# Draining a fused decoder layer: where the shared expert's pieces, the last routing groups and the packet sends stand

## The chip, the cores and the metric

One core of one Trainium2 chip. The metric is device time of one launch in microseconds (us): the kernel before took 727.16 us as the median of 3 runs (726.34 to 728.71). The core has five engines that run side by side and wait for each other through semaphores: TensorE (PE, matmuls; its weight loads are listed as PEld), VectorE (DVE), ScalarE (ACT), GpSimd (POOL) and SyncE (SP). SP, ACT and POOL start DMAs.

## The reference, cut to what matters

`x` is 32 sequences (B) of 128 rows (S) of 256 channels (D), all float32.

```python
x = layernorm(x + self_attention(x))          # 16 heads of 16 channels, causal
x = layernorm(x + retention(x, ctx))          # rotated q and k, decay mask, no softmax
hs = silu(x @ sw1[:, :256] + b) * (x @ sw1[:, 256:] + b)      # the shared expert, for every row
shared = hs @ sw2 + sb2
probs = softmax(x @ gate_w + gate_b)          # 8 experts; each row takes the best 2
routed = sum over the row's 2 experts of  p_e * expert_e(x)   # same shape as the shared expert
x = layernorm(x + shared + routed)
```

## The kernel before, in words

**Attention steps.** A token block `t` is one of the 32 sequences (128 rows). Both attentions run in a software pipeline of steps `n`. In step `n` each engine handles several blocks at different stages: scores and softmax of block n, weighing of the values and first layernorm of block n-2 (result `x1`), keys, values and queries of the second attention for block n-3 (`K_TURNED`, `XV`, `Q_TURNED`; VectorE makes `products` of them, GpSimd adds these to `rot`), its 128x128 scores `SCX` and its output `YX` for n-4 with the second layernorm (`packets`, that is x2), and for n-5 the turned x2 (`x2T`) and its gate logits (`GATE`, added up to `gc`). From step 32 = B on no new block comes, and the steps run out: step 32 is the first without scores, step B+4 = 36 the last with any attention work. The order of instructions on each engine is the order in which the `step` functions write them; there is no planner.

**Routing groups.** Blocks are gated in `GROUPS`: seven groups of 4 (q0 to q6: blocks 0 to 27), then two of 2 (q7: 28 and 29, q8: 30 and 31). A group's VectorE work has four parts (L1556 to L1562): largest and lowered logits; sums and top two probabilities; top two experts and `picks`; `places` and `positions`. `groups_at(n, lag)` gives the groups whose part `lag` stands in step n: part 0 in `group_step(q)`, which is 32, 34 and 36 for q6, q7 and q8, and each further part one step later, so `places` of q8 stands in step 39. TensorE computes the group's prefix counts (L996 to L1004) in the step of `places`. `places` also moves `base`, the next free row of each expert's region in the HBM tensor `sent`; only after q8 is it final.

**Sending.** GpSimd scatters each block's packets (x2 and routing data) with two indirect DMAs per block to `sent` (L641). `sent_at(n)` sends one block per step, for blocks up to 27; the pairs 28, 29 and 30, 31 go in steps 38 and 40. The sends stand in front of the step's `rot` additions and of the layernorms' `rstd` (L650, L654).

**Shared expert.** Rows 0 to 15 (four quarters q of 4 blocks, `EARLY`) go through the shared expert here. `shared_hidden(q, f, bank)` is 4 matmul calls of 512 columns in two halves (a and b) in PSUM banks `bank` and `bank+1`; ScalarE makes silu of one half, VectorE `shared_gate` (L1452) the product, then `shared_output(q, ...)` has 8 calls of 256 columns and `add_shared` (L1463) adds the result to `kept`. `shared_between(n)` lays one of these pieces into each of steps 33 to 39 on TensorE, in the middle of the step: hidden(0,0), (0,1), (1,0), output 0, hidden (1,1), (2,0), output 1. Behind the loop come hidden (2,1), (3,0), (3,1) and outputs 2 and 3. Each engine has its own `shared_between`.

**Behind the steps.** VectorE makes `tail_rows` from `base` and then a plan of 15 small steps (`tile_expert`, `tile_row`), with one `shared_gate` in the middle. After `tail_rows` SP and ACT write 128 zero rows behind each expert's region (5 and 3 DMAs). SP waits for the plan, for all sends and for the zero rows (L550 to L554); then it starts the loads of the routed tiles: tile i reads 128 packets from `sent` into `xg`. There are 71 tiles. Per tile TensorE turns `xg` (L1038), makes the hidden layer (L1051) and the result of the tile before (L1060). SP also stores `kept` (L547) between the loads of tiles 2 and 3. A last stage joins everything, makes the shared expert of the other rows and the third layernorm.

Of the kernel before, what the change touches and what calls it, by code (L numbers as in the profile page):

```python
# [14 lines left out]
P = 128  # L15
# [71 lines left out]
def groups_at(n, lag):  # L87
    return [q for q in range(len(GROUPS)) if group_step(q) + lag == n]


def sent_at(n):

    return [lo + j for q, (lo, size) in enumerate(GROUPS) for j in range(size)
            if group_step(q) + 4 + (j if size == 4 else 0) == n]


def decoder_kernel(nc, x, ctx_turned, wqkv, xwq, xwk, xwv, gate_w, gate_b, sw1, sb1, sw2, sb2,
                   rw1, biases, rw2, table_f32, table_bf16, x_turned, x_blocks, out):
    ctx = ExitStack()
    with ctx:  # L100
# [26 lines left out]
        GATE = ps[:, 7, D:D + NE]  # L127
        PREFIX = ps[:, 7, D + NE:D + 5 * NE].rearrange("p (b e) -> p b e", e=NE)
# [279 lines left out]
        FIRST_STEP, END_STEP = -2, group_step(len(GROUPS) - 1) + 5  # L408
# [190 lines left out]
        def _(eng):  # L599
# [17 lines left out]

            def step(n):
# [18 lines left out]
                for t in sent_at(n):  # L637
                    eng.wait_ge(pos_set, group_of(t) + 1)
                    eng.wait_ge(scored, 4 * min(n + 1, B))
                    for j in range(TOPK):  # L640
                        eng.indirect_dma_start(sent, bass.IndirectOffsetOnAxis(ap=pos[:, t, j:j + 1], axis=0),  # L641
                                               packets[:, t % SLOTS, :], None).then_inc(sent_in[t % SLOTS], 16)
# [92 lines left out]
        def _(eng):  # L735
# [96 lines left out]
            def shared_hidden(q, f, bank):  # L832
                if q > 0:
                    eng.wait_ge(sgh_set, 2 * (q - 1) + f + 1)
                for half in range(2):
                    shared_half(q, f, half, bank)

            def shared_output(q, *banks):

                eng.wait_ge(sgh_set, 2 * q + 2)  # L840
                for i, bank in enumerate(banks):
                    if 0 < q < EARLY - 1:
                        eng.wait_ge(sy_added, 2 * (q - 1) + i + 1)
                    for b in (2 * i, 2 * i + 1):
                        for c in range(FFN // P):
                            mm = eng.matmul(ps[:, bank, b % 2 * D:(b % 2 + 1) * D], sgh[:, q % 2, c, b * P:(b + 1) * P],
                                            sw2_sb[:, c, :], start=(c == 0), stop=(c == FFN // P - 1))
                    mm.then_inc(sy_made, 1)

            def shared_between(n):  # L850

                if n == B + 1:
                    eng.wait_ge(ffn_in, 16 * (2 + 2 * NE))
                    eng.wait_ge(expd, 4 * B)
                    shared_hidden(0, 0, 0)
                if n == B + 2:
                    shared_hidden(0, 1, 2)
                if n == B + 3:
                    shared_hidden(1, 0, 0)
                if n == B + 4:  # L860
                    eng.wait_ge(pT_set, 4 * B)
                    eng.wait_ge(att_set, B)
                    shared_output(0, 4, 5)
                if n == B + 5:
                    shared_hidden(1, 1, 2)
                if n == B + 6:
                    shared_hidden(2, 0, 0)
                if n == B + 7:
                    shared_output(1, 4, 5)
# [7 lines left out]
            def step(n):  # L877
# [20 lines left out]
                if live(t):  # L898
# [4 lines left out]
                    eng.wait_ge(x1T_set, t + 1)  # L903
# [19 lines left out]
                if live(t):  # L923
# [4 lines left out]
                    else:  # L928
                        eng.wait_ge(res2_set, n - 4)
                    for m in range(2):  # L930
# [16 lines left out]
                shared_between(n)  # L947
# [26 lines left out]
                if live(n - 1):  # L974
                    turn_probs(n - 1, 3)
                t = n - 5
# [8 lines left out]
                if n == 0:  # L985
# [4 lines left out]
                    project_k(NG - 1, 0, 5)  # L990
                for q in groups_at(n, 3):
# [15 lines left out]
                if live(t):  # L1007
# [4 lines left out]
                    after(eng, gc_set, n - 4)  # L1012
                    for c in range(DC):
                        mm = eng.transpose(TR[:, c * P:(c + 1) * P], x1[:, t % 2, c * P:(c + 1) * P], ident)
# [8 lines left out]
            shared_hidden(2, 1, 2)  # L1023
            shared_hidden(3, 0, 0)
# [88 lines left out]
        def _(eng):  # L1113
# [23 lines left out]
            def shared_between(n):  # L1137
                if n == B + 1:
                    eng.wait_ge(heads_made, B)
                    shared_silu(0, 0, 0)  # L1140
                if n == B + 2:
                    shared_silu(0, 1, 2)
                if n == B + 3:
                    shared_silu(1, 0, 0)
                if n == B + 5:
                    shared_silu(1, 1, 2)
                if n == B + 6:
                    shared_silu(2, 0, 0)

            def step(n):  # L1150
# [26 lines left out]
                shared_between(n)  # L1177
# [13 lines left out]
                if live(t):  # L1191
                    eng.wait_ge(x1_turned, t + 1)
                    after(eng, xq_made, t - 1)
                    eng.copy(x1T[:, t % 2, :, :].rearrange("p c t -> p (c t)"), TR).then_inc(x1T_set, 1)
# [15 lines left out]
            shared_silu(2, 1, 2)  # L1210
# [103 lines left out]
        def _(eng):  # L1314
# [150 lines left out]
            def shared_between(n):  # L1465
                if n == B + 1:
                    shared_gate(0, 0, 0)
                if n == B + 2:
                    shared_gate(0, 1, 2)
                if n == B + 3:  # L1470
                    shared_gate(1, 0, 0)
# [299 lines left out]
```

## Time and profile before

| | |
|---|---|
| median of 3 runs | 727.16 us |
| the profiled execution | 723.76 us |
| its span in the trace | 721.7 us |
| PE, DVE, ACT, POOL busy | 683.2, 489.2, 478.9, 343.1 us |
| matmul records of the routed tiles, L1051 and L1060 | 138.9 and 74.9 us |

The profiled execution is 2.06 us longer than its span and 3.40 us shorter than the median. Times in the trace count from the start of the span. A float32 matmul call stands as two records, so a `shared_hidden` is 8 records and a `shared_output` 16. "Busy" of PE counts records, which overlap a little. A gap ahead of an instruction is given in brackets with the instruction that ended it.

### The profile page before, as it was taken

To read this page: it belongs to the slowest core of one execution; us is meant where nothing else is said; L and a number is where in the kernel's file an instruction comes from. 1 tells how busy PE (TensorE), PEld (TensorE's weight loads), DVE (VectorE), ACT (ScalarE), POOL (GpSimd) and SP (SyncE) were. 2 spreads that over 40 slices of the span, in tenths; PEclk is the share of its full clock that TensorE was granted. 3 is DMA by queue.
4 is the path that set the end of the run, shared out by engine and by line. 5 is a ranking of instruction groups with operands and counts; after the bars stand their busy time and mean duration, and the time that the engine had idled before them with its cause. 6 is when DMAs were issued, how large, how long until landed. Compare 5 with 4: busy or idle time off the path is not lost.

```text
span 721.7 us, 21540 instructions
## 1 busy us (share of the span) xinstructions
PE 683.2 (95%) x6174; PEld 588.5 (82%) x6175; DVE 489.2 (68%) x1563; ACT 478.9 (66%) x1319; POOL 343.1 (48%) x469
## 2 busy tenths in 40 slices
PE   7989999999999999999998899889999999999994
PEld 5868888888888888888887555779999999998653
DVE  3666878888888888888896376445555555554266
ACT  0367888888888888888884242356666666666256
POOL 1001323435645455454455355055665556556495
PEclk9999999999999999999999899999999999999998
DMA  8743367424523233232336024686777777777597
GB/s 306 236 146 114 116 204 240 137 88 147 158 88 96 67 91 105 86 107 83 104 97 198 31 89 143 198 221 126 140 134 139 133 139 136 135 137 130 124 349 261
DMA packets 93947, 104.30 MB, mean 145 GB/s; under 512 B 13200, under 2 KB 86672, under 8 KB 92976
## 3 DMA queue, kind: packets, MB, share of 16 engines
q1 hardware_dynamic: 78480, 79.43, 37.2%
q0 software_dynamic: 14688, 23.26, 16.4%
q8 instruction: 40, 0.66, 0.4%
q10 hardware_dynamic: 704, 0.66, 0.3%
q14 instruction: 35, 0.29, 0.1%
HBM read 62.21 MB, written 41.10 MB: 143 GB/s over the span
## 4 chain that ended last, share of the span: by engine, by line
PE 78%; DVE 5%; DMA 5%; POOL 4%; issue 4%; SPq 3%; ACT 1%; DVEq 0%; POOLq 0%; ACTq 0%
PE ps L1051 15%; PE ps L1060 8%; PE ps L806 6%; PE ps L908 5%; PE ps L794 5%; PE ps L816 4%; PE ps L771 4%; PE ps L739 4%; PE ps L911 4%; PE ps L774 4%; PE ps L932 4%; DMA xg<-sent 3%; POOL first_use L715 2%; PE ps L1038 2%; PE ps L826 2%
## 5 line engine op out<-in xcount | busy, mean ns | idle before, releaser
L1118 ACT ACTIVATE prob<-ps,nmax 128x128 f32<-128x128 f32 x512 | 147.0, 380 | 27.4 <-DVE nmax L1332 27.4
L1051 PEld LDWEIGHTS ps<-xgT,attn_only 128*128 128x128 f32 x1136 | 136.0, 192 | 7.4 <-DVE ghT L1614 2.2
L1051 PE MATMUL ps<-xgT,attn_only 128*128 128x128 f32 x1136 | 138.9, 275 | 1.1 <-ACT xgT L1230 1.1
L674 POOL DMA_INDIRECT total<-rot,result_row x71 | 111.6, 1572 | 36.8 <-issue 34.3
L1332 DVE TENSOR_REDUCE nmax<-ps 128x4 f32<-128x512 f32 x128 | 82.2, 685 | 17.7 <-PE ps L794 17.0
L1614 DVE SCALAR_TENSOR_TENSOR ghT<-ps,attn_only 128x128 f32<-128x128 f32 x142 | 43.3, 347 | 71.0 <-PE ps L1051 59.3
L615 POOL TENSOR_TENSOR rot<-products 128x128 f32<-128x128 f32 x128 | 61.3, 499 | 57.1 <-DVE products L1342 57.0
L1125 ACT COPY pT<-ps 128x512 f32<-128x512 f32 x124 | 74.4, 600 | 20.8 <-PE ps L806 16.4
L806 PE MATMUL ps<-tf,prob 128*128 128x128 f32 x512 | 77.9, 275 | 4.4 <-DVE pT L1447 3.3
L641 POOL DMA_INDIRECT sent<-packets,pos x64 | 63.6, 993 | 35.6 <-PE ps L794 20.9
L1060 PE MATMUL ps<-first_use,ghT 128*128 x284 | 74.9, 386 | 0.0
L806 PEld LDWEIGHTS ps<-tf,prob 128*128 128x128 f32 x512 | 58.7, 140 | 11.0 <-issue 4.9
L1238 ACT COPY attn_only<-first_use 128x512 f32 x71 | 44.0, 619 | 28.4 <-issue 28.4
L826 PE MATMUL ps<-prob,sw_sb 128*128 128x512 f32 x128 | 56.8, 594 | 0.0
L1230 ACT COPY xgT<-ps 128x256 f32<-128x256 f32 x71 | 26.5, 373 | 44.7 <-PE ps L1038 43.9
L1060 PEld LDWEIGHTS ps<-first_use,ghT 128*128 128x128 f32 x284 | 48.4, 190 | 6.0 <-issue 0.5
L1342 DVE TENSOR_TENSOR products<-ps,tf 128x256 f32<-128x256 f32 x128 | 46.4, 404 | 6.7 <-PE ps L911 2.3
L1603 DVE COPY attn_only<-first_use 128x512 f32 x71 | 31.2, 439 | 28.4 <-issue 28.0
L654 POOL TENSOR_TENSOR rstd<-mv,neg_half 128x1 f32<-128x1 f32 x32 | 17.7, 552 | 67.0 <-DVE mv L1350 67.0
L1224 ACT ACTIVATE attn_only<-ps,attn_only 128x128 f32<-128x128 f32 x142 | 44.2, 361 | 7.6 <-PE ps L1051 4.8
L662 POOL TENSOR_TENSOR weight<-weight_part,xg 128x1 f32<-128x1 f32 x71 | 13.4, 188 | 70.4 <-ACT rot L1244 49.9
L826 PEld LDWEIGHTS ps<-prob,sw_sb 128*128 128x128 f32 x128 | 23.9, 190 | 26.0 <-issue 25.6
(143 smaller groups left out, 1408.1 us busy)
## 6 DMA issues: line engine op xcount, KB each, us to landing
xg<-sent SPq DMA_DIRECT2D x71, 130.5 KB, 2.1
attn_only<-in_L_ffn_rb SPq DMA_DIRECT2D x71, 130.0 KB
first_use<-total SPq DMA_DIRECT2D x12, 512.0 KB, 8.7
total<-zeros POOLq DMA_DIRECT2D x3, 1408.0 KB, 8.0
k_dram<-first_use SPq DMA_DIRECT2D x4, 1024.0 KB, 4.6
attn_only<-in_x_turned SPq DMA_DIRECT2D x32, 128.0 KB, 2.5
attn_only<-k_dram SPq DMA_DIRECT2D x256, 16.0 KB
attn_only<-in_x SPq DMA_DIRECT2D x32, 128.0 KB, 2.7
```

The costliest lines, as they stand in the source:

```text
L615: eng.tensor_tensor(rot[:, t % 2, m + e, :], ra[:, t % 2, m + e, :], rb[:, t % 2, m + 1 - e, :], ALU.add).then_inc(done, 1)
L641: eng.indirect_dma_start(sent, bass.IndirectOffsetOnAxis(ap=pos[:, t, j:j + 1], axis=0), packets[:, t % SLOTS, :], None).then_inc(sent_in[ ...
L674: eng.indirect_dma_start(totals[slot % 2], bass.IndirectOffsetOnAxis(ap=result_row[:, slot:slot + 1], axis=0), yw[:, slot, :], None, compu ...
L806: mm = eng.transpose(PROBT[:, n * P:(n + 1) * P], prob[:, t % 2, 4 * u + n, :], ident)
L826: mm = eng.matmul(ps[:, bank + half, :].rearrange("p (b t) -> p b t", b=QB), sw1_sb[:, c, cols:cols + P], x2T4[:, q % EARLY, :, c, :], sta ...
L1051: mm = eng.matmul(ps[:, 2 * r + half, f * P:(f + 1) * P], w_now[:, r, c, cols:cols + P], xgT[:, r, c, :], start=(c == 0), stop=(c == DC - 1))
L1060: mm = eng.matmul(ps[:, 4 + r, 0:D], ghT[:, r, c, :], rw2_sb[:, bass.ds(e * (FFN // P * D) + c * D, D)], start=(c == 0), stop=(c == FFN // ...
L1118: ins = eng.activation(prob[:, t % 2, 4 * u + n, :], SCORE[u][:, n * P:(n + 1) * P], ACT.Exp, bias=nmax[:, t % 2, 4 * u + n:4 * u + n + 1])
L1125: eng.copy(pT[:, u, :, :].rearrange("p n t -> p (n t)"), PROBT).then_inc(pT_set, 1)
L1224: eng.activation(sil[:, r, f, :], ps[:, 2 * r, f * P:(f + 1) * P], ACT.Silu, bias=side[:, slot, f:f + 1]).then_inc(sil_set, 1)
L1332: eng.tensor_reduce(nmax[:, t % 2, 4 * u:4 * u + 4], SCORE[u].rearrange("p (h j) -> p h j", j=P), AX_X, ALU.max, negate=True).then_inc(max ...
L1342: eng.tensor_tensor(into[:, t % 2, m:m + 2, :], source, table[:, m:m + 2, :], ALU.mult).then_inc(done, 1)
```

## The change

Three things are moved; the arithmetic stays the same, and so does the number of matmuls, gating operations, silus and sends.

1. **Groups.** For q6, q7 and q8 the parts stand 0, 1, 1 and 2 steps behind `group_step`: the second and third part share a step, `places` and the prefix counts come in steps 34, 36 and 38 (before 35, 37, 39). The loop ends one step earlier.
2. **Sends.** Blocks 20 and 21 are sent in step 32, 22 and 23 in 33, 24 and 25 in 34, 26 and 27 in 35, 28 and 29 in 36, 30 and 31 in 38. From step 34 on the sends stand at the end of GpSimd's step, behind `rot` and `rstd`.
3. **Pieces of the shared expert.** TensorE gets two places per step: `shared_upper` behind SCX, where `shared_between` stood, and `shared_lower` behind the gate logits. Halves a and b of one hidden piece are parted. So hidden(0,0) stands in step 32; hidden (0,1), (1,0), (1,1) each have one half up and one down in steps 33, 34, 35; output 0 stands in step 36 in two parts, one of them between the turning of x2 and the gate logits; hidden(2,0) in 36 and 37, (2,1) in 37 and 38; output 1 and hidden(3,0) in 39. Behind the loop only hidden(3,1) and outputs 2 and 3 are left. On ScalarE the silu moves behind the x1 copy, on VectorE the gate product moves ahead of the second residual sum, and in the plan `add_shared(1)` and `shared_gate(3, 0, 0)` stand where `shared_gate(2, 1, 2)` stood. The turned x1 of blocks 30 and 31 goes to PSUM bank 4 instead of bank 7, so it no longer waits for the gate logits, and the step's waits are changed to match.

```diff
+QUICK = len(GROUPS) - 3
+LAST_SENT = {B: (20, 21), B + 1: (22, 23), B + 2: (24, 25), B + 3: (26, 27), B + 4: (28, 29), B + 6: (30, 31)}
 def groups_at(n, lag):
-    return [q for q in range(len(GROUPS)) if group_step(q) + lag == n]
+    return [q for q in range(len(GROUPS)) if group_step(q) + (lag if q < QUICK else (0, 1, 1, 2)[lag]) == n]
 def sent_at(n):
-    return [lo + j for q, (lo, size) in enumerate(GROUPS) for j in range(size)
-            if group_step(q) + 4 + (j if size == 4 else 0) == n]
+    if n < B:
+        return [t for t in (n - 12,) if 0 <= t < LAST_SENT[B][0]]
+    return LAST_SENT.get(n, ())
...
-        FIRST_STEP, END_STEP = -2, group_step(len(GROUPS) - 1) + 5
+        FIRST_STEP, END_STEP = -2, group_step(len(GROUPS) - 1) + 4
...
 # GpSimd: send(n) holds the old loop over sent_at(n)
+                if n < B + 2:
+                    send(n)
...
+                if n >= B + 2:
+                    send(n)
...
 # TensorE
+            def shared_first(q, f, bank):
+                if q > 0:
+                    eng.wait_ge(sgh_set, 2 * (q - 1) + f + 1)
+                shared_half(q, f, 0, bank)
+            def shared_rows(q, i, bank):
+                eng.wait_ge(sgh_set, 2 * q + 2)
+                if 0 < q < EARLY - 1:
+                    eng.wait_ge(sy_added, 2 * (q - 1) + i + 1)
+                for b in (2 * i, 2 * i + 1):
+                    for c in range(FFN // P):
+                        mm = eng.matmul(...)
+                mm.then_inc(sy_made, 1)
+            def shared_upper(n):
                 if n == B + 1:
+                    shared_first(0, 1, 2)
+                if n == B + 2:
+                    shared_first(1, 0, 0)
+                if n == B + 3:
+                    shared_first(1, 1, 2)
+                if n == B + 4:
+                    eng.wait_ge(pT_set, 4 * B)
+                    eng.wait_ge(x1T_set, B)
+                    eng.wait_ge(att_set, B)
+                    shared_rows(0, 0, 4)
+                if n == B + 5:
+                    shared_half(2, 0, 1, 0)
+                    shared_first(2, 1, 2)
+                if n == B + 6:
+                    shared_half(2, 1, 1, 2)
+                if n == B + 7:
+                    shared_output(1, 4, 5)
+                    shared_hidden(3, 0, 0)
+            def shared_lower(n):
+                if n == B:
                     eng.wait_ge(ffn_in, 16 * (2 + 2 * NE))
                     eng.wait_ge(expd, 4 * B)
                     shared_hidden(0, 0, 0)
+                if n == B + 1:
+                    shared_half(0, 1, 1, 2)
                 if n == B + 2:
+                    shared_half(1, 0, 1, 0)
                 if n == B + 3:
+                    shared_half(1, 1, 1, 2)
                 if n == B + 4:
+                    shared_first(2, 0, 0)
...
-                    eng.wait_ge(x1T_set, t + 1)
+                    if t < B - 2:
+                        eng.wait_ge(x1T_set, t + 1)
+                    else:
+                        eng.wait_ge(gc_set, n - 5)
...
+                if n == B + 4:
+                    shared_rows(0, 1, 5)
...
-                        mm = eng.transpose(TR[:, c * P:(c + 1) * P], x1[:, t % 2, c * P:(c + 1) * P], ident)
+                        mm = eng.transpose(turned_x1(t)[:, c * P:(c + 1) * P], x1[:, t % 2, c * P:(c + 1) * P], ident)
...
-            shared_hidden(2, 1, 2)
-            shared_hidden(3, 0, 0)
             shared_hidden(3, 1, 2)
...
 # VectorE, in the plan behind the loop
-            shared_gate(2, 1, 2)
+            add_shared(1, 4, 5)
+            shared_gate(3, 0, 0)
```

## Rows read from the trace of the kernel before

**Rows 1.** Windows: engines' busy us (records), granted clock, DMA share, GB/s.

```profile
391.20:404.20 13.00, 10.22 (x79) 6.91 (x77) 6.49 (x22) 4.16 (x8) 6.08 (x10) 0.96 0.41 139
404.20:410.20 6.00, 6.00 (x24) 5.62 (x25) 3.20 (x13) 0.37 (x1) 3.57 (x5) 0.52 0.19 68
410.20:422.40 12.20, 10.71 (x46) 5.58 (x45) 6.26 (x31) 4.73 (x7) 4.09 (x7) 1.00 0.15 54
422.40:437.90 15.50, 15.04 (x63) 9.91 (x61) 8.97 (x47) 4.53 (x6) 10.94 (x12) 1.00 0.27 96
437.90:455.25 17.35, 17.35 (x61) 10.74 (x60) 12.02 (x29) 3.28 (x5) 5.79 (x6) 1.00 0.48 138
```

**Rows 2.** Chain that ended last, around the first routed tiles: start, us, what.

```profile
438.75 1.28 DVE kept L1463 x2
440.03 0.37 DVE tail_rows L1578
447.20 3.46 DMA sent<-zeros
450.80 0.28 SPq L561
...
462.41 3.34 DMA xg<-sent
```

**Rows 3.** Timeline of TensorE: start, us, line, operation, gap and its releaser.

```profile
390.75 0.41 PE L1014 MATMUL ps<-tf,x 128*128 128x128 f32 x2 [1.27 <-DVE gc L1543]
396.13 3.60 PE L826 MATMUL ps<-prob,sw_sb 128*128 128x512 f32 x8
402.11 0.61 PE L981 MATMUL ps<-gate_w_sb,x2T 128*128 128x8 f32 x4 [1.73 <-ACT x2T L1183]
...
437.86 0.17 PE L996 MATMUL ps<-picks,tb 128*128 128x16 bf16 x1
...
448.35 7.07 PE L846 MATMUL ps<-sw_sb,sgh 128*128 128x256 f32 x32
455.25 0.38 PE L1038 MATMUL ps<-tf,xg 128*128 128x128 f32 x2
...
465.79 0.44 PE L1038 MATMUL ps<-tf,xg 128*128 128x128 f32 x2 [1.85 <-DMA xg<-sent]
```

**Rows 4.** Timeline of ScalarE (first row) and VectorE: the same columns.

```profile
399.81 1.28 ACT L1135 ACT_TABLE_LOAD   x1 [5.27 <-PE ps L826]
...
404.19 0.18 DVE L1366 TENSOR_REDUCE gsum<-gexp 128x4 f32<-128x32 f32 x1
405.45 0.73 DVE L1452 SCALAR_TENSOR_TENSOR sgh<-ps,sb_sb,pT 128x512 f32<-128x512 f32 x1
...
417.70 0.08 DVE L1389 MATCH_VALUE_LOAD top_i<-top_p,gprob 128x8 f32 x1
...
418.95 0.19 DVE L1413 TENSOR_TENSOR picks<-pick 128x32 bf16<-128x32 f32 x1
```

**Rows 5.** GpSimd: L641's durations (ns) and landings (us), then its timeline.

```profile
L641 POOL DMA_INDIRECT sent<-packets,pos x64: 959/970/1076, 161.9 to 444.5; - x64
DMA to landing us min/median/max: 2.5/3.1/5.8
...
416.02 0.57 POOL L654 TENSOR_TENSOR rstd<-mv,neg_half 128x1 f32<-128x1 f32 x1 [4.62 <-DVE mv L1350]
...
425.41 1.02 POOL L641 DMA_INDIRECT sent<-packets,pos  x1 [1.26 <-DVE pos L1436]
...
444.53 0.97 POOL L641 DMA_INDIRECT sent<-packets,pos  x1 [0.30 <-issue]
```

**Rows 6.** Timeline: GpSimd and VectorE side by side, and VectorE with GpSimd sending.

```profile
392.04 0.73 POOL L635 TENSOR_TENSOR x2b<-packets,sb_sb 128x256 f32<-128x256 f32 x1 [0.53 <-DVE packets L1555]
392.09 0.73 DVE L1360 TENSOR_TENSOR gs<-gc,lmax 128x32 f32<-128x32 f32 x1
...
427.86 0.18 DVE L1360 TENSOR_TENSOR gs<-gc,lmax 128x16 f32<-128x16 f32 x1
```

More of the change, by code:

```diff
@@ L616, in turn_into, with send @@
                                       ALU.add).then_inc(done, 1)
+            def send(n):
+                for t in sent_at(n):
+                    eng.wait_ge(pos_set, group_of(t) + 1)
+                    eng.wait_ge(scored, 4 * min(n + 1, B))
+                    for j in range(TOPK):
+                        eng.indirect_dma_start(sent, bass.IndirectOffsetOnAxis(ap=pos[:, t, j:j + 1], axis=0),
+                                               packets[:, t % SLOTS, :], None).then_inc(sent_in[t % SLOTS], 16)
             def step(n):
@@ L636, in step @@
                                       sb2_sb[:, :], ALU.add).then_inc(x2b_set, 1)
[L637 to L642, printed above, removed]
+                if n < B + 2:
+                    send(n)
                 t = n - 3
@@ L830, in shared_half, with shared_hidden @@
                     mm.then_inc(shid_made, 1)
-            def shared_hidden(q, f, bank):
+            def shared_first(q, f, bank):
                 if q > 0:
                     eng.wait_ge(sgh_set, 2 * (q - 1) + f + 1)
-                for half in range(2):
-                    shared_half(q, f, half, bank)
+                shared_half(q, f, 0, bank)
+            def shared_hidden(q, f, bank):
+                shared_first(q, f, bank)
+                shared_half(q, f, 1, bank)
+            def shared_rows(q, i, bank):
[4 more added lines that the diff above has]
+                    for c in range(FFN // P):
+                        mm = eng.matmul(ps[:, bank, b % 2 * D:(b % 2 + 1) * D], sgh[:, q % 2, c, b * P:(b + 1) * P],
+                                        sw2_sb[:, c, :], start=(c == 0), stop=(c == FFN // P - 1))
+                mm.then_inc(sy_made, 1)
@@ L838, in shared_output @@
             def shared_output(q, *banks):
-                eng.wait_ge(sgh_set, 2 * q + 2)
                 for i, bank in enumerate(banks):
[L842 to L848, printed above, removed]
@@ L850, in shared_between @@
-            def shared_between(n):
-                if n == B + 1:
+                    shared_rows(q, i, bank)
+            def shared_upper(n):
+                if n == B + 1:
+                    shared_first(0, 1, 2)
[16 more added lines that the diff above has]
+                    shared_hidden(3, 0, 0)
@@ L1193, in step @@
                     after(eng, xq_made, t - 1)
-                    eng.copy(x1T[:, t % 2, :, :].rearrange("p c t -> p (c t)"), TR).then_inc(x1T_set, 1)
+                    eng.copy(x1T[:, t % 2, :, :].rearrange("p c t -> p (c t)"), turned_x1(t)).then_inc(x1T_set, 1)
+                shared_between(n)
                 if live(n) and live(n + 1):
@@ L1474, in shared_between @@
                 if n == B + 5:
-                    shared_gate(1, 1, 2)
+                    shared_gate(2, 0, 0)
                 if n == B + 6:
-                    shared_gate(2, 0, 0)
-                if n == B + 7:
-                    add_shared(1, 4, 5)
+                    shared_gate(2, 1, 2)
             def step(n):
@@ L1523, in step @@
                     eng.bn_stats(bn1[:, r2, :], res1[:, r2, :]).then_inc(bn1_set, 1)
+                if n == B + 1:
+                    shared_gate(0, 0, 0)
+                if n == B + 2:
+                    shared_gate(0, 1, 2)
+                if n == B + 3:
+                    shared_gate(1, 0, 0)
+                if n == B + 4:
+                    shared_gate(1, 1, 2)
                 if live(t4):
```

48 lines of the change are left out of this document (20 added, 28 removed).

## The prediction

> **What bounds the kernel now.** I read the windows first: where does TensorE lose time? Behind step 31 it loses it in one place only, the running out of the steps. From 391.20 to 404.20 it is busy 10.22 of 13.00 us; from 404.20 to 410.20 it is busy throughout, but its clock was granted at 0.52, so it ran at the lower of its two levels (1.2 of 2.4 GHz) after a stretch with long gaps; from 410.20 to 422.40 it is busy 10.71 of 12.20; from 422.40 on it has almost no gap, and from 437.90 to 455.25 none [rows 1]. Then the timeline of TensorE, for what ended these gaps: 1.27 us for the logits' copy in front of the turned x1, 1.73 us for a turned x2 [rows 3]. ScalarE made that x2 late because it had waited 5.27 us for a whole hidden piece and then loaded an activation table for 1.28 us [rows 4].
>
> Last the chain of waits, for what the routed tiles wait for. It does not run through TensorE. It runs from `places` of the last group over `add_shared(1)` (1.28 us), `tail_rows` (ends 440.40), SP's zero rows (the last one starts at 447.20 and lands 3.46 us later) to the first load, which SP begins at 450.80, and on to tile 3, whose packets land at 465.79 [rows 2]. TensorE ends its own shared pieces at 455.25 and goes on without a gap, but at tile 3 it stands 1.85 us for SP's load [rows 3]. So two paths meet: TensorE's, with 1.85 us of slack at tile 3, and SP's, which sets the start of the routed tiles. Behind tile 3 the change touches nothing, and a shift there passes to the end.
>
> **The change part by part.** *Work on TensorE.* A hidden piece takes 3.46 us: three fill 437.96 to 448.35 (one alone is 8 records, 3.60 us with its drain); an output takes 3.45, since two fill 448.35 to 455.25 [rows 3]. In front of the prefix counts of q8 stood five hidden pieces and two outputs; now six and one. That is the same work. What can go is only lost time: gaps of 1.27, 2.78, 1.49 and 0.46 us, plus 0.48 of 6.0 us and 0.04 of 13.0 us for the clock, 3.4 us; 9.4 us in all [rows 1, 3]. This is the upper bound of TensorE's gain.
>
> *New waits.* I laid the new order by hand, instruction by instruction, with the durations of this trace, from 389.4, where the logits of block 27 end and hidden(0,0) now follows. Its input landed before that. It runs to 392.9, over the old gap of 1.27. Four things then cost:
> - Steps 32 and 33 send two blocks each: two more sends each, at 1.27 us from start to start (970 ns and 0.30 of idle [rows 5]), so `rot` and `rstd` stand 2.5 us further back in GpSimd's queue. In step 32 this makes x1 of block 30 1.3 us late, which hidden(0,0) covers; in step 33 the additions for block 30 end at 401.3 and TensorE asks for them at 406.
> - In step 33 the second and third part of q6 stand together on VectorE, 1.26 and 1.44 us (404.19 to 405.45, 417.70 to 419.14 [rows 4]). They end at 407.0, and the products of block 31 stand behind them. TensorE is ready for SCX of block 30 at 406.05 and starts at 407.85: a gap of 1.8 us.
> - Prefix counts of q6 end at 413.45; the next SCX shares their bank and waits for `base`, 1.05 us.
> - In step 34 the sends of blocks 24 and 25 start with q6's positions at 415.0 (before: 425.41 [rows 5]) and hold GpSimd to 420.1. The last `rstd` of all, for block 31, is ready to start at 418.8 but now has these sends and the x2 sum in front: it runs 420.9 to 421.45 (0.57 us [rows 5]). TensorE stands 0.55 us for x2 of block 31, and VectorE's q7 chain ends at 424.1, before TensorE asks at 426.25.
>
> With 0.5 us of short waits TensorE loses 3.9 us where it lost 9.4: 5.5 us less. The schedule itself puts the prefix of q8 at 431.75, against 437.86 [rows 3]: 6.1 less. I take the middle, 5.8. The parted outputs in step 36 and the late silus cost nothing: each gate product is asked for one step after it is made, and the halves between cover it.
>
> *SP's path.* Behind `positions` of q8 stood `add_shared(1)`, 1.28 us; now stands a gate product of 0.75 us [rows 2, 4]. So `tail_rows` comes 5.8 + 0.5 = 6.3 us earlier, at 434.1. Three things must not be late next. The plan: its middle now waits for silu(3,0), whose matmuls end at 438.9; with silu 0.7, product 0.75 and five more steps of 2.2 us it ends at 442.5. The sends: before, 16 of them ran in one chain from 425.41 to 445.5; now only four follow the last positions, 432.9 to 438.0, and with the longest landing seen, 5.8 us [rows 5], they are in at 443.8. The zero rows: 440.40 to 450.66 becomes 434.1 to 444.4 [rows 2]. The zero rows stay last, by 0.6 us.
>
> *End of the shared pieces.* Behind the loop three pieces instead of five; with the pieces of step 39 TensorE reaches the first routed tile near 449.5, 5.8 us earlier. It would ask for tile 3 at 458.1; SP's load lands at 465.79 - 6.3 = 459.5. SP's stores of `kept` need `add_shared(3)`, at 450.7; SP comes to them at 451.1.
>
> **Sum.** SP's path sets the start: 6.3 us, of which I take 6.2 for the near tie of the stores. The profiled execution took 723.76 us (span 721.7), so one like it takes 717.6 (715.5). The median of the runs lies 3.40 us above that execution; from it, 727.16 - 6.2 = **721.0 us**.
>
> *A rule against it.* VectorE's lowering of logits took 0.73 us while GpSimd's sum was running, and 0.18 (at half the size) while GpSimd was only sending [rows 6]; the 64 sends took 959 to 1076 ns, whatever VectorE did [rows 5]. The Trainium skill (SBUF — State Buffer, "Who interferes with whom") says that VectorE and GpSimd take one shared port pair as an exclusive lock, and that descriptors of a DMA sent by GpSimd can't be written while VectorE holds it in a two-port mode. The first row agrees. On sends the trace speaks against a loss; by the rule, sends moved beside VectorE's busiest steps would stretch, which is part of the first rival.
>
> **Rivals.**
> - *GpSimd becomes the bound.* The four sends in front of the last `rstd` are on the path. If each is held for one VectorE operation of 0.73 us, that is 2.9 us: 723.9. For it: only these sends have no slack, and my 415.0 hangs on q6's positions. Against it: 64 sends within 0.12 us of each other [rows 5]. The skill's port rule, in the page named above, is one way to it.
> - *Waits move, they don't go.* VectorE, not TensorE, becomes the clock of steps 33 to 36, since its groups got denser; my 3.9 us of loss doubles and adds the clock's 2.9 again. Gain 6.2 - 3.9 - 2.9 below zero is the far end; with the doubling and half of the clock it is 0.8: 726.4, no change.
> - *All gaps fill.* If VectorE keeps up and GpSimd's sends start earlier, TensorE loses about 1 us: gain 8.9 with the 0.5, and the sends (slack 0.6 us against the zero rows) then limit it near 8.5: 718.7.
> - *Slower: the clock falls in step 34.* The trace shows it once: 0.96 to 404.20, with the gap of 1.73 us and shorter ones in it, then 0.52 for 6 us [rows 1, 3]. The new order has its longest gap, 1.8 us, at 406. If the clock falls there and stays low for the 9.0 us of matmuls of step 34 and the start of 35, those take 18: 721.0 + 9.0 = 730.0. It decides from 8.4 us of such work on (6.2 and the 0.3% below). Against it: between the gaps the halves of the shared pieces now stand, and before, 1.27 us alone did not lower the clock.
>
> That it doesn't do what it says I see no room for.
>
> **How the numbers follow.** Forecast 0.56 (its own range 719.4 to 723.0), GpSimd 0.13, waits that move 0.10, all gaps 0.12, slower 0.09. A difference under 0.3%, 2.2 us, can't be told from none. Faster by more: 0.56 + 0.13 + 0.12, 0.81. Same 0.10; slower 0.09. For 8 in 10 the range must hold the first two cases and most of the third: 717.5 to 725.0.
>
> **What would show it.** Right: `tail_rows` about 6 us earlier, near 434; first load 6 us earlier; clock at 1.00 through 404 to 410; a gap near 1.8 us ahead of SCX in step 34 with VectorE's products as releaser; `rstd` of block 31 directly behind four sends; still a gap at tile 3. Wrong: a stretch at 0.5 clock, `tail_rows` later than 437, or a first load that now waits for sends or plan rather than zero rows. If tile 3 starts 6 us earlier but the end does not, the routed stage took the gain back.

## The result and the profile after

The changed kernel took **721.69 us** as the median of 8 runs (720.38 to 724.33), the kernel before, on the same chip, 727.54 (724.37 to 729.93): ratio 0.9912, 95% interval 0.9887 to 0.9937. The forecast was 721.0. Two more measurements of the same pair gave 0.9873 (0.9838 to 0.9907) and 0.9878 (0.9842 to 0.9914). The profiled execution took 721.88 us, span 719.9.

The windows of TensorE answer to [rows 1]; the columns are length, busy us (records), granted clock, DMA share, GB/s.

```profile
380.00:390.00 10.00, 8.56 (x86) 0.83 0.63 182
390.00:400.00 10.00, 8.71 (x73) 1.00 0.56 187
400.00:410.00 10.00, 7.58 (x36) 1.00 0.16 56
410.00:420.00 10.00, 8.60 (x51) 1.00 0.08 27
420.00:430.00 10.00, 9.44 (x43) 1.00 0.27 95
430.00:440.00 10.00, 10.00 (x39) 1.00 0.35 124
```

The stretch at half clock at 404 to 410 is gone; in its place stands a shorter fall at 383 to 387, in front of the change's steps. TensorE's timeline answers to [rows 3]:

```profile
382.72 0.18 PE L1042 MATMUL ps<-picks,tb 128*128 128x32 bf16 x1 [1.44 <-DVE gc L1593]
...
392.26 0.41 PE L1005 MATMUL ps<-tf,packets 128*128 128x128 f32 x2 [1.29 <-DVE scx L1556]
402.31 0.66 PE L959 MATMUL ps<-tf,oT 128*128 128x128 f32 x4 [1.70 <-issue]
404.55 0.68 PE L988 MATMUL ps<-rot 128*128 128x128 f32 x4 [0.69 <-DVE products L1392]
414.26 0.68 PE L988 MATMUL ps<-rot 128*128 128x128 f32 x4 [1.33 <-DVE products L1392]
420.53 0.68 PE L988 MATMUL ps<-rot 128*128 128x128 f32 x4 [0.57 <-DVE base L1474]
427.63 0.44 PE L1005 MATMUL ps<-tf,packets 128*128 128x128 f32 x2
...
454.55 0.38 PE L1087 MATMUL ps<-tf,xg 128*128 128x128 f32 x2
464.80 0.44 PE L1087 MATMUL ps<-tf,xg 128*128 128x128 f32 x2 [1.76 <-DMA xg<-sent]
```

Only the gaps of 1.33, 0.57 and 1.76 us were in the forecast. Then VectorE, SyncE and the chain of waits (its piece `sent<-zeros`), which answer to [rows 2]:

```profile
438.72 0.22 DVE L1628 TENSOR_SCALAR tail_rows<-base,tf 128x8 uint32<-128x8 f32 x1
444.96 0.69 DVE L1513 TENSOR_TENSOR kept<-ps,kept 128x512 f32<-128x512 f32 x1 [2.09 <-remote]
448.42 0.22 DVE L1647 TENSOR_TENSOR tile_row<-tile_f,tf 1x71 int32<-1x71 f32 x1
...
440.53 7.23 SPq L551 DMA_DIRECT2D sent<-zeros  x5
450.30 0.37 SPq L571 DMA_DIRECT2D xg<-sent  x1
...
447.42 2.00 DMA sent<-zeros
```

`tail_rows` came 1.2 us earlier than before, not 6; tile 3 by 1.0. Yet the runs had gained 6. So this trace, or the one of before, held something that is not the change. To compare traces I count from one fixed place ahead of the change, the prefix counts of q5 (first line of the TensorE rows; 380.93 in the first trace of before, 382.72 here).

### The profile page after: what moved, and what is told of

The parts are those of the page before. It is cut to its first block, busy times and chain, and to the rows that moved or that the text cites. A ratio compares the mean times of both kernels' runs of the same rounds, so it can differ in the third digit from the quotient of the medians.

```text
span 719.9 us, 21546 instructions
## 1 busy us (share of the span) xinstructions
PE 682.0 (95%) x6174; PEld 587.2 (82%) x6175; DVE 488.0 (68%) x1563; ACT 478.6 (66%) x1319; POOL 342.8 (48%) x469
## 4 chain that ended last, share of the span: by engine, by line
PE 73%; issue 7%; DMA 5%; DVE 5%; POOL 4%; SPq 3%; ACT 1%; another core or an unknown queue 1%; DVEq 0%; POOLq 0%; ACTq 0%
PE ps L1100 15%; PE ps L1109 8%; PE ps L821 6%; PE ps L809 5%; PE ps L949 5%; PE ps L831 4%; PE ps L786 4%; PE ps L789 4%; PE ps L975 4%; PE ps L952 4%; PE ps L754 3%; DMA xg<-sent 2%; POOL first_use L730 2%; PE ps L1087 2%; PE ps L959 2%
## 5 line engine op out<-in xcount | busy, mean ns | idle before, releaser
L667 POOL TENSOR_TENSOR rstd<-mv,neg_half 128x1 f32<-128x1 f32 x32 | 17.6, 549 | 62.5 <-DVE mv L1400 62.5
L663 POOL TENSOR_TENSOR rstd<-mv,neg_half 128x1 f32<-128x1 f32 x32 | 18.0, 562 | 54.1 <-DVE mv L1400 54.1
```

## Experiments

Twelve measurements. The first four and the last four ran on one chip, the middle four on another; which one ran the first result isn't known. Each has its own ratio to before from the same chip, and only ratios are compared between chips (the expected times of experiments 5 to 8 were written with the first result's 721.7 in mind). This table counts from the prefix counts of q5, us. "Stall" is a stretch, at some 430 to 450, in which SyncE, VectorE and ScalarE go on late, all at once (experiment 5 and the last section):

| kernel | to tail_rows | to tile 3 | clock low at 382 to 388 | stall |
|---|---|---|---|---|
| before, first trace | 59.0 | 84.9 | no | no |
| before, second trace | 62.9 | 88.0 | no | yes |
| changed, first | 56.0 | 82.1 | yes | yes |
| changed, second | 52.5 | 78.0 | yes | no |
| changed, third | 56.1 | 82.1 | yes | yes |
| pieces alone, twice (1, 11) | 51.0; 53.0 | 81.5; 83.3 | no; yes | yes; yes |
| pieces, plan first (12) | 51.0 | 81.0 | no | yes |
| pieces and groups (4) | 58.5 | 83.5 | no | yes |
| experiments 6; 8 | 52.5; 52.5 | 76.6; 78.5 | yes; yes | no; no |
| experiment 7 | 50.9 | 75.1 | no | no |

**1. Only the pieces.** The new places of the shared expert's halves and bank 4, with the groups and sends of before. Against the changed kernel:

```diff
 def groups_at(n, lag):
...
+    return [q for q in range(len(GROUPS)) if group_step(q) + lag == n]
...
-                if n == B + 7:
-                    shared_output(1, 4, 5)
-                    shared_hidden(3, 0, 0)
...
+            shared_output(1, 4, 5)
+            shared_hidden(3, 0, 0)
             shared_hidden(3, 1, 2)
```

> Only the third part of the change: the shared expert's halves in their new places and the turned x1 of blocks 30 and 31 in bank 4; groups and sends as before. Output 1 and hidden(3,0) stand behind the loop, so that the prefix counts of the last group have the same work in front of them as in both kernels (six hidden pieces, one output). Theory A (the gain is TensorE's lost time in steps 32 to 36, filled by the halves): 5 to 6.5 us faster than before, ratio 0.991 to 0.993, first gap in step 34 smaller than with the dense groups. Theory B (the gain is that the last group is gated a step earlier): no gain, ratio 0.998 to 1.002.

Measured: 721.44 us, 0.9894 (0.9871 to 0.9917): the whole effect, from one of the three parts, and a little more than theory A's 0.991 to 0.993. The gap ahead of SCX in step 34 is 0.57 us where the changed kernel has 1.33, as theory A says.

**2. Only the groups.** Against the kernel before:

```diff
 def groups_at(n, lag):
-    return [q for q in range(len(GROUPS)) if group_step(q) + lag == n]
+    return [q for q in range(len(GROUPS)) if group_step(q) + (lag if q < QUICK else (0, 1, 1, 2)[lag]) == n]
```

> Only the first part: q6, q7 and q8 gated in fewer steps; pieces and sends as before. Theory A: tail_rows still stands behind add_shared(1) and output 1, so nothing comes earlier, and VectorE's denser steps cost up to 1.8 us: ratio 1.000 to 1.003. Theory B: prefix counts stand one output (3.45 us) earlier, about 3 us faster, ratio 0.995 to 0.997.

Measured: 737.81 us, 1.0111 (1.0078 to 1.0145), slower, which neither theory had. TensorE's timeline and its windows:

```profile
421.79 1.19 PE L947 MATMUL ps<-rot 128*128 128x128 f32 x4 [2.08 <-DVE base L1426]
422.77 5.71 PE L828 MATMUL ps<-prob,sw_sb 128*128 128x512 f32 x8
...
416.00:422.00 6.00, 3.19 (x21) 0.85 0.06 22
422.00:428.00 6.00, 6.00 (x12) 0.58 0.21 69
```

The prefix counts now stand directly in front of SCX, which waits for `base`; behind that gap a hidden piece takes 5.71 us where it took 3.60 [rows 3], at a granted clock of 0.58.

**3. Groups and sends, no pieces.** Experiment 2 and, besides:

```diff
 def sent_at(n):
+    if n < B:
+        return [t for t in (n - 12,) if 0 <= t < LAST_SENT[B][0]]
+    return LAST_SENT.get(n, ())
...
+                if n >= B + 2:
+                    send(n)
```

> First and second part without the third. Theory A: no gain over groups alone; with no half behind the logits of step 32, the two more sends there (2.5 us) delay x1 of block 30 in the open by 1.3 us: ratio 1.000 to 1.004. Theory B: 3 to 6 us faster, ratio 0.992 to 0.996. A third theory, that the late sends held the first load, also says faster here, by up to 3 us.

Measured: 727.75 us, 0.9984 (0.9959 to 1.001). The second fall of the clock stays (a hidden piece of 5.91 us behind a gap of 1.61). Without the pieces the other two parts give nothing, as theory A said.

**4. Pieces and groups, old sends.** The changed kernel with the `sent_at` of before and all sends in front of `rot` and `rstd`:

```diff
-                if n < B + 2:
-                    send(n)
+                send(n)
...
-                if n >= B + 2:
-                    send(n)
```

> The change without its second part: the sends stay one block a step, the last at the end. Theory A: the last 16 sends then run as one chain of 20.3 us from step 36 on (about 426) and end near 446, with 3 to 5 us to land: later than the zero rows by 4 us or more, so the first load waits for sends and the kernel is 3 to 5 us slower than the changed one, ratio to before 0.996 to 1.000. Rival (the sends have slack in any order): as the changed kernel, ratio 0.991 to 0.993.

Measured: 724.59 us, 0.994 (0.9916 to 0.9964). This lies between theory A's range and the rival's, and the trace doesn't show theory A's cause, a first load that waits for sends. The loss stands ahead of `tail_rows`, 58.5 us behind q5's counts: TensorE's prefix counts of q8 ended at 432.2, and VectorE's `place`, which needs them, began only at 438.97, in the stall. The clock is at 1.00 from 382 on: with the halves in place the gaps of 1.33 and 0.97 us ahead of the two SCX do not lower it. The theory that the earlier gating of the last groups brings the gain (theory B of experiments 1 to 3) has fallen; that the pieces bring it stands.

**5. The changed kernel again, unchanged.**

> The changed kernel once more, unchanged, for its trace. Open: in its first trace, while GpSimd's sends ran, SyncE, VectorE and ScalarE all slowed down at once (SyncE's zero rows 7.23 us of issuing where the kernel before took 5.74; add_shared(1) waited 2.09 us for a semaphore; the plan ended 9.7 us behind tail_rows where 8.4 was forecast). Theory S (the order of sends and zero rows in this kernel causes it): it stands at the same place, 441 to 445 us, zero rows 6.9 to 7.5 us of issuing, median 721 to 722. Theory C (it is a chance event of one execution): the zero rows take 5.6 to 6.0 us here, or the stall lies elsewhere; from tail_rows to the first load 10.4 us (before) instead of 11.6, and the profiled execution is 1 to 2 us shorter than the first one's 719.9 us of span.

Measured: 715.12 us, 0.9873. VectorE, SyncE and TensorE, in this order:

```profile
433.37 0.22 DVE L1628 TENSOR_SCALAR tail_rows<-base,tf 128x8 uint32<-128x8 f32 x1
442.42 0.22 DVE L1647 TENSOR_TENSOR tile_row<-tile_f,tf 1x71 int32<-1x71 f32 x1
434.99 5.43 SPq L551 DMA_DIRECT2D sent<-zeros  x5
444.19 0.37 SPq L571 DMA_DIRECT2D xg<-sent  x1
408.96 0.68 PE L988 MATMUL ps<-rot 128*128 128x128 f32 x4 [1.34 <-DVE products L1392]
449.19 0.38 PE L1087 MATMUL ps<-tf,xg 128*128 128x128 f32 x2
458.86 0.44 PE L1087 MATMUL ps<-tf,xg 128*128 128x128 f32 x2 [1.17 <-DMA xg<-sent]
```

This order of instructions can run without the stall (theory C): the zero rows take 5.43 us of issuing, not 7.23, and `add_shared(1)` no longer waits. But this is another chip, and experiment 10 has the stall again. The profiled execution took 717.93 us, 2.8 above the median of its kernel.

**6. Tile 3's load first.** `load(3, 3)` stands ahead of the four `store_kept`.

```diff
+            load(3, 3)
             for q in range(EARLY):
                 store_kept(q)
-            load(3, 3)
```

> SyncE issues the load of tile 3 before the four stores of kept blocks that stood in front of it. Theory: tile 3's gap of 1.76 us on TensorE ends with that load; the stores before it cost SyncE their wait for add_shared(3) and four issues, some 1.5 us. With the load first, the gap falls below 0.4 us and the time by 1.0 to 1.8 us: 720 beside 721.7. Rival: the stores are not what the load waits for (its packets land late because the queue is full of the loads of tiles 0 to 2, 3.46 us each): the gap stays above 1.3 us and the time is the same. Second rival: TensorE, 1.8 us earlier at tile 3, finds tile 4's load late instead, and the gap only moves.

Measured: 716.29 us, 0.9892 (0.9866 to 0.9918), the same as experiment 5. TensorE:

```profile
457.13 0.38 PE L1087 MATMUL ps<-tf,xg 128*128 128x128 f32 x2
461.12 0.44 PE L1087 MATMUL ps<-tf,xg 128*128 128x128 f32 x2 [0.95 <-DMA xg<-sent]
465.48 0.43 PE L1087 MATMUL ps<-tf,xg 128*128 128x128 f32 x2 [1.23 <-DMA xg<-sent]
470.42 0.44 PE L1087 MATMUL ps<-tf,xg 128*128 128x128 f32 x2 [1.70 <-DMA xg<-sent]
```

Tile 3 has no gap; tiles 4, 5 and a later one have. The second rival holds: the gap only moves. Summed over all 71 tiles TensorE stands 4.67 us for loads, 3.84 in experiment 5.

**7. Three edits together:** experiment 6, the plan's 15 steps in one row ahead of `add_shared(1)`, four zero-row transfers on SyncE instead of five.

```diff
-        TAILS_SP = 5
+        TAILS_SP = 4
...
-            add_shared(1, 4, 5)
-            shared_gate(3, 0, 0)
             planned(eng.tensor_scalar(tile_e[:, :], tile_f[:, 0, :], float(NE - 1), None, ALU.min))
...
+            add_shared(1, 4, 5)
+            shared_gate(3, 0, 0)
             shared_gate(3, 1, 2)
```

> Three edits together: tile 3's load first; VectorE runs the 15 steps of the plan without the additions of output 1 and a gate product in their middle; four zero-row transfers instead of five on SyncE's queue behind tail_rows (one more on another queue). Theory: from tail_rows to the first load it was 11.6 us, bounded by plan (9.7 from tail_rows) and zero rows (7.2 of issuing and 2.0 to land). With the plan at 7.7 us (15 steps, VectorE alone) and one transfer less (1.1 us), the first load comes 1.5 to 2.5 us earlier; the product behind the plan makes hidden(3,0)'s output late by at most 1 us, which TensorE's routed start does not see. Time: 718.0 to 720.0 (721.7 less 1 to 1.8 for tile 3 and less 1 to 2). Rival: TensorE's own shared pieces bound the start of the routed tiles (no gap before tile 0 in the changed kernel), so the earlier load gives nothing beyond tile 3's gap: same time as the run with the load first alone.

Measured: 717.3 us, 0.9895 (0.9862 to 0.9927): no better. The last step of the plan started at 437.95, 5.5 us behind `tail_rows`, but the first load did not come earlier: it started 11.1 us behind `tail_rows` where experiment 5 has 10.8. So the run doesn't test an earlier load. It does bear out the rival in another way: TensorE reached tile 0 at 448.30 without a gap, and the chain of waits runs through its own pieces from 431.13 to 448.46. From q5's counts to the end this trace is 1.5 us shorter than experiment 5's (333.5 and 334.9), which the fall of the clock, absent here, covers.

**8. Paced sends.** From block 24 on GpSimd waits until the packets of block t-2 have landed.

```diff
+                    if t >= 24:
+                        eng.wait_ge(sent_in[(t - 2) % SLOTS], 32 * ((t - 2) // SLOTS + 1))
```

> From block 24 on GpSimd sends block t only when block t-2's packets have landed, so that at most four sends are under way at once. Theory Q (the slowing of SyncE, VectorE and ScalarE comes from many sends of GpSimd under way together): no stretch in which SyncE's sequencer instructions take 0.7 us each, zero rows at 5.6 to 6.0 us of issuing, but GpSimd's sends end later: landing took up to 5.8 us, four sends take 5.1 to issue, so each pair waits 1 to 3 us and the last packets land some 5 us later than 443.8 to 446; the first load then waits for them, up to 2 us slower than the changed kernel, 722 to 724. Rival (the slowing comes from something else, such as instruction fetches): the slow stretch is still there in the trace, and the time is 722 to 725 as well.

Measured: 717.66 us, 0.9903 (0.9874 to 0.9932). No stall here, but there was none in any trace of this chip. And the added wait held nothing back: the last eight sends ran from 428.56 to 438.72, in 10.16 us, as without it (428.14 to 438.30). The 1 to 3 us of waiting per pair that were expected did not come, so the edit changed nothing and the run says nothing on the stall's cause.

**9. The kernel before again, for a second trace.** (The text's 981.98 is a slip for 381.98.)

> The kernel before once more, for a second trace beside the changed one on one chip. Open: its first trace (723.76 us) lay 3.4 us under its own median, and the ratio gave the change 6.4 and then 9.2 us where 6.2 was forecast from that one trace. Theory M (that execution was a low one; a usual one loses 2 to 4 us more, in front of the steps that the change touches or in them): this trace shows tail_rows behind weigh of block 30 later than the 58.0 us of the first (981.98 to 439.95 read as 381.98 to 439.95), or a stretch before 382 longer by 2 to 4 us. Rival (the forecast's sum was too low: the change gives 8 to 9 us against any execution): the stages of this trace last as in the first one to within 1 us, and the changed kernel stands 8 to 9 us under it.

Measured: 727.35 us beside 729.45 of its twin, 0.9984 (0.9964 to 1.0005). TensorE, VectorE and GpSimd:

```profile
438.39 0.17 PE L996 MATMUL ps<-picks,tb 128*128 128x16 bf16 x1
449.29 5.40 PE L826 MATMUL ps<-prob,sw_sb 128*128 128x512 f32 x8 [3.68 <-DVE sgh L1452]
443.31 0.17 DVE L1421 TENSOR_TENSOR place<-ps,base 128x16 f32<-128x16 f32 x1 [4.40 <-remote]
444.28 0.96 POOL L641 DMA_INDIRECT sent<-packets,pos  x1 [3.33 <-DVE pos L1436]
```

TensorE had ended the prefix counts of q8 at 438.6; VectorE began `place` at 443.31. In the first trace of before `place` began at 438.14, 0.3 us behind the start of the counts [rows 3]. From q5's counts to `tail_rows` it is 62.9 us, not 59.0; at tile 3 3.1 of these 3.9 us are left, and at the end 2.0, since TensorE stands less for loads behind it (1.82 us in all, against 5.56). Theory M holds, with two sources: the span is 3.3 us longer than the first, 2.0 of it behind q5's counts, from the stall, and 1.3 ahead of them, whose cause isn't shown.

**10. The changed kernel a third time.**

> The changed kernel a third time, beside the kernel before and the two pieces-only kernels. If the slowing of SyncE, VectorE and ScalarE in its first trace was a chance event, this trace has tail_rows 55 us behind turn_x's stage as the second one had (weigh of block 30 to tail_rows 51.5 us), zero rows of 5.4 to 5.8 us of issuing and tile 0 at weigh + 67.3. If it belongs to the kernel, 60 us and 7 us.

Measured: 720.11 us, 0.9878 (0.9842 to 0.9914), to `tail_rows` 56.1 us (from weigh of block 30 54.8, not 51.5). ScalarE, TensorE and SyncE:

```profile
399.48 0.59 ACT L1205 COPY oT<-ps 128x512 f32<-128x512 f32 x1 [3.36 <-remote]
400.12 0.66 PE L959 MATMUL ps<-tf,oT 128*128 128x128 f32 x4 [1.44 <-issue]
438.33 7.16 SPq L551 DMA_DIRECT2D sent<-zeros  x5
```

Both losses of the first trace are back, the late copy of the heads (experiment 5 has it at 395.87, with 0.67 us of idle time in front) and the slow zero rows. So they are no single chance event: two of the three traces of this kernel have them, and only that of experiment 5, on the second chip, is free of them.

**11. Only the pieces, again.**

> Only the pieces (halves of the shared expert's pieces spread over steps 32 to 36, bank 4 for the last turned x1), a second time. Its first run took 0.9894 of before where the whole change had taken 0.9912 in other runs. Theory P (the groups and the sends add nothing): 0 to 1.5 us of the whole change beside it here, and with SyncE's slow stretch (10.2 us for the five zero rows) gone its trace ends earlier: first load behind tail_rows 11 to 13 us instead of 16.2. Rival (the groups and sends are worth 1 to 3 us once no stall hides it): 16 sends in one chain to the end hold the first load back, slower than the whole change by 1 to 3 us.

Measured: 720.63 us, 0.9888 (0.9855 to 0.9922), beside 720.11 of the whole change. Theory P on the time; but the stall came here too (zero rows 10.12 us), so what groups and sends are worth without it isn't settled.

**12. The pieces, and the plan in one row.** Experiment 1 with the second part of experiment 7's diff.

> Only the pieces, and VectorE runs the 15 steps of the plan without the additions of output 1 and a gate product in their middle. In the pieces-only trace the plan ended 15.1 us behind tail_rows since it waited for output 1, and TensorE stood 1.5 and 1.8 us for the additions and a product. Theory: plan ends 5.5 us behind tail_rows; the first load then waits for the last send, which starts 8.8 us behind tail_rows and lands 1.5 to 5.8 us later: 11 to 16 us; TensorE's own pieces end at 448.7 with no gap if the additions come at the plan's end. Time 0 to 2 us under the pieces alone, and within 1 us of the whole change. Rival (the additions are now late for output 2, which takes their banks): a gap of 1 us or more there, and the time is that of the pieces alone or above.

Measured: 720.76 us, 0.9897 (0.9862 to 0.9932). VectorE and SyncE:

```profile
432.58 0.22 DVE L1623 TENSOR_SCALAR tail_rows<-base,tf 128x8 uint32<-128x8 f32 x1
438.01 0.22 DVE L1640 TENSOR_TENSOR tile_row<-tile_f,tf 1x71 int32<-1x71 f32 x1
435.49 10.30 SPq L550 DMA_DIRECT2D sent<-zeros  x5
448.29 0.37 SPq L570 DMA_DIRECT2D xg<-sent  x1
```

The plan was ready 5.4 us behind `tail_rows`, as expected; the first load, 15.7 us behind, waited for zero rows issued in a stall. A gap of 1.52 us for the additions stood ahead of an output, as the rival says, and the time is that of the pieces alone.

No kernel beat the changed one beyond its interval.

## Why the prediction held

**The sum.** Forecast 6.2 us, from one execution to another; measured 5.9 between the medians, 6.4 by the ratio, and by the ratios of experiments 5 and 10 some 9. The traces that carry the stall on both sides differ by the same 5.9 at tile 3 (88.0 and 82.1), and those without it by 6.9 (84.9 and 78.0). From q5's counts to `tail_rows` the forecast was 59.0 - 6.3 = 52.7; the second trace of the changed kernel, which has no stall, shows 52.5. Its q5 counts stand within 0.04 us of those in the first trace of before, so its times can be read beside the forecast's: `tail_rows` ends at 433.59 (forecast 434.1), the plan at 442.64 (442.5), and tile 0 starts at 449.19 (449.5), tile 3 at 458.86 (459.5).

**Partly by errors that cancel.** The forecast let TensorE lose 3.9 us. Where the clock doesn't fall at 384 (experiment 7) the way to `tail_rows` is 50.9, a gain of 8.1 where 6.3 was forecast. Three gaps were sized too large, by 1.5 us together: ahead of SCX in step 34 1.33 for 1.8 (VectorE's releaser was right), 0.57 for 1.05 at `base`, none for 0.55 at x2 of block 31. Against that stands the fall of the clock at 384, 1.6 us (52.5 against 50.9), which the forecast had not. It stands in all three traces of the changed kernel and in experiments 2, 6, 8 and 11, but not in 1, 3, 4, 7 and 12 nor in either trace of before; it lies in front of all steps of the change. So on TensorE's side the rival "all gaps fill" (8.9 us) was nearer than the forecast. That a whole execution without the fall gains the rival's 8.5 us isn't shown: there is no such trace of the changed kernel.

**What the first trace hid.** To `tail_rows` it has 56.0, 5.1 more than 50.9: 1.6 for the clock, 2.2 for the heads' copy and the products behind it (gaps of 1.70 and 0.69, where experiment 5 has one of 0.15), 1.0 for the longer gap at 392.26 (0.25 in experiment 5). The third trace has such losses again (gaps of 1.44 and 0.70, and 1.08 at 388 to 390), so the usual gain is smaller than the clean one. But before, too, loses where it has a stall: 3.9 us to `tail_rows` that my trace of it didn't show. I put the difference to the median, 3.40 us, on both kernels as a constant. The second trace of before shows that 2.0 of some 3.3 us come from a stall in the steps of the change, and it was luck that the constant nearly holds for the changed kernel too.

**The clock** was at 1.00 through 404 to 410, as forecast: in each of the ten traces with the pieces, and in none of the four without. Slower by a falling clock, the rival with 0.09, did not come, but experiments 2 and 3 show it at just the place it named (step 34, behind a gap of 1.6 to 2.1 us, 5.7 to 5.9 us for a hidden piece) as soon as the halves are taken out. With the halves and the same groups it does not fall there (experiment 4), so what the forecast said against it, the halves between the gaps, is what decided.

**GpSimd.** `rstd` of block 31 ran directly behind four sends and the x2 sum, in the trace after:

```profile
424.92 0.96 POOL L632 DMA_INDIRECT sent<-packets,pos  x1 [0.30 <-issue]
425.90 0.65 POOL L652 TENSOR_TENSOR x2b<-packets,sb_sb 128x256 f32<-128x256 f32 x1
426.49 0.57 POOL L667 TENSOR_TENSOR rstd<-mv,neg_half 128x1 f32<-128x1 f32 x1
```

TensorE did not stand for it: x2 of block 31 was turned at 427.63 without a gap, since output 0's first part covered it. The eight sends of these steps took 0.96 to 1.03 us, all 64 a median of 968 ns (before 959 to 1076 [rows 5]), so the rival "GpSimd becomes the bound" falls. One send took 1286 ns; it began 0.3 us behind VectorE's comparison `passed` in the plan, which has two operands in SBUF:

```profile
440.61 0.75 DVE L1637 TENSOR_TENSOR passed<-counts,tf 128x568 f32<-128x568 f32 x1
440.91 1.29 POOL L632 DMA_INDIRECT sent<-packets,pos  x1 [0.30 <-issue]
```

So it is in all ten traces with the pieces: the send that begins 0.3 us into this comparison takes 1.28 or 1.29 us, and its neighbours 0.96. An exclusive lock on a port pair that VectorE and GpSimd share is what the Trainium skill states (SBUF — State Buffer, "Who interferes with whom"). These ten sends agree with such a lock, at 0.32 us each, off the path that decides.

**SyncE's path.** That the zero rows stay last was right (the chain of experiment 5 has them too). That it sets the start of the routed tiles was wrong in the first trace after and in experiments 5 to 8, where TensorE comes to tile 0 from its own pieces without a gap. Its 1.85 us at tile 3, on which this rested, aren't slack that an earlier load gives back: with that load earlier the gaps stand at the next tiles and the time is the same (experiments 6 and 7). Whether an earlier first load would give anything was not tested, since in experiment 7 it came no earlier. It did no harm to the number, since both paths came some 6 us earlier.

**The parts.** The forecast counted all three parts as one schedule. The pieces alone give the whole of it (0.9894 and 0.9888); the groups alone cost 8 us (1.1%); groups and sends together are neutral. One reason why they add nothing shows on the way to `tail_rows`: with the clock's fall in both, the pieces alone take 53.0 us (experiment 11) and the whole change 56.0 and 56.1. Some 2 us of that are the late copy of the heads, which is later in the changed kernel (last section).

## What to carry to other kernels

Where a pipeline runs out, first fill the emptying engine with independent work in halves small enough to stand in each gap; moving the dependent chain up makes the vector engine denser and opens gaps of its own. Take two or three traces of the kernel before as well: its single profile lay 3 us from the usual execution, in good part for a reason inside the stretch that was to be changed. A gap in front of one transfer is worth nothing to mend when the next transfers on that queue only take it over. Before a run is read as a test, see in its trace whether the edit did what it was meant to (in experiment 7 it did so only in part, in 8 not at all).

## What the runs showed of the hardware that was not expected

**Three engines slow down together.** In some executions, while GpSimd's indirect sends run one behind the other, SyncE, VectorE and ScalarE get their semaphores late at the same time. In the chain of the first trace after:

```profile
441.24 0.70 SPq L550
441.97 0.69 issue
```

each small instruction of SyncE takes 0.7 us, where such pieces are 0.05 to 0.63 us in experiment 5. In experiment 1 it lasts 10 us, on SyncE, VectorE and ScalarE:

```profile
435.20 10.17 SPq L550 DMA_DIRECT2D sent<-zeros  x5
443.89 0.69 DVE L1508 TENSOR_TENSOR kept<-ps,kept 128x512 f32<-128x512 f32 x1 [7.12 <-PE ps L860]
443.99 1.27 ACT L1179 ACTIVATE pT<-ps,sb_sb 128x512 f32<-128x512 f32 x2 [13.07 <-remote]
```

GpSimd's sends and TensorE's matmuls kept their own durations. For VectorE the stall ends 0.8 to 2.4 us behind the end of a chain of sends (chain's end, then the first VectorE instruction released: 440.9 and 443.3 in experiment 9, 436.7 and 439.0 in 4, 442.1 and 443.9 in 1, 445.2 and 447.0 in 11, 442.4 and 444.2 in 12, 447.5 and 448.4 in 2, 441.3 and 442.9 in 10). ScalarE can come free sooner, at 436.8 in experiment 4 and 437.4 in 9. The stall stands in seven of the eight traces of one chip and in none of the four of the other. The eighth, experiment 3, is the only one whose last 16 sends stand in runs of four; the others have 8 to 12 in a row. But the second chip has 8 in a row too, and the first trace of before 16, without a stall. That the sends cause it is argued from this coincidence and not shown; what chooses the execution and the chip is open.

**A late copy without a busy releaser.** In two of three traces of the changed kernel ScalarE's copy of the heads began some 3 us after the matmuls that it needed had ended (3.02 and 2.75); in the third it followed them at once. It goes with the sends that run at that time: with the changed kernel's four in a row it is 3.02 and 2.75 us late, and with the two of the old order 1.6, in experiments 1, 4, 11 and 12. Experiment 4 differs from the changed kernel in the sends alone:

```profile
396.67 0.58 ACT L1201 COPY oT<-ps 128x512 f32<-128x512 f32 x1 [2.22 <-remote]
```

Behind it TensorE stands 0.30 us, in the changed kernel 1.70 and 1.44, and 0.5 more for the products. Where no send ran when the matmuls ended (both traces of before, experiments 2 and 3) the copy was at once, 0.1 us behind them; on the second chip it was at once even beside four sends. So it looks like a small stall of the same kind, and the change's own sends seem to lengthen it; the cause isn't shown here either.

**The clock can fall or not, behind the same gap.** At 381 to 387 it fell in seven of the fourteen traces, with and without the pieces, groups and sends of the change, behind a gap of 1.44 us; in the seven others, behind the same gap, it did not. A stage that takes 1.08 us at full clock then takes 1.93 (the weighing, at 383.94 in the first trace after). What chooses isn't shown.
